# An attention and mixture-of-experts layer on one core: the first batch's scores after half the query projection, the second half's projections over three batches, two norms and all softmax normalisations on GpSimd

## What is computed

```python
x = x + attention(layernorm(x), ctx, Wq, Wkv, Wout)
x = x + ffn(layernorm(x), gate, gate_up, down, shared_gate_up, shared_down)

def attention(q, latent, Wq, Wkv, Wout):
    qp = q @ Wq.T                                  # 8 x 112 x 512
    k, v = split(latent @ Wkv.T)                   # latent is 8 x 375 x 128
    scores = einsum("bhqd,bhkd->bhqk", qh, kh) / sqrt(32)
    scores = where(tril, scores, lowest)           # row q sees keys 0..q, so 112 keys do
    attn = softmax(scores)
    return (attn @ vh) @ Wout.T
```

## Time and profile before

| | |
|---|---|
| median of 3 runs | 339.84 us (339.09 to 340.3) |
| the profiled execution | 340.88 us |
| its span, first to last instruction | 339.0 us |
| busy: PE, DVE, ACT, POOL | 323.1, 268.6, 232.4, 143.3 us |
| granted TensorE clock, mean | 0.991 |

### The profile page before, as it was taken

How to read it: one execution, slowest core, us unless ns; L and a number is a source line. 1 busy time by engine, 2 the same in 40 slices (tenths; PEclk the granted TensorE clock), 3 DMA queues, 4 the chain that set the end, 5 groups by cost and what they waited for, 6 DMA issues and landing times.

```text
span 339.0 us, 7041 instructions
## 1 busy us (share of the span) xinstructions
PE 323.1 (95%) x2285; PEld 279.3 (82%) x2285; DVE 268.6 (79%) x677; ACT 232.4 (69%) x582; POOL 143.3 (42%) x151
## 2 busy tenths in 40 slices
PE   7999998999999999999999999899999999999990
PEld 7898876777786798889888978789989999999980
DVE  4889779999756176876667998899999999999940
ACT  4666999999844134131225788788899899989830
POOL 3335475888842000352500005557772432432463
PEclk9999999999999999999999999999999999999996
DMA  7999300000005699598699965554455455556243
GB/s 227 380 338 380 139 3 3 3 3 3 0 2 198 248 367 370 237 300 289 224 271 253 251 244 98 102 117 104 90 111 131 90 96 125 114 92 113 50 48 45
DMA packets 32227, 53.03 MB, mean 156 GB/s; under 512 B 7488, under 2 KB 15808, under 8 KB 31168
## 3 DMA queue, kind: packets, MB, share of 16 engines
q1 hardware_dynamic: 24912, 43.31, 39.2%
q0 software_dynamic: 4576, 9.23, 15.9%
q10 hardware_dynamic: 2704, 0.04, 0.5%
HBM read 32.24 MB, written 16.92 MB: 145 GB/s over the span
## 4 chain that ended last, share of the span: by engine, by line
PE 74%; ACT 8%; DVE 5%; DMA 5%; POOL 3%; issue 2%; SPq 1%; POOLq 1%; DVEq 0%; ACTq 0%
PE bank L583 26%; PE bank L913 22%; PE bank L940 5%; ACT prob L1076 4%; PE bank L644 3%; PE bank L944 3%; PE bank L807 2%; PE bank L950 2%; PE bank L954 2%; DMA w_sg<-sguT 2%; DMA act_w<-act_e 2%; DMA w_kv<-wkvT 1%; PE bank L793 1%; PE bank L575 1%; PE bank L655 1%
## 5 line engine op out<-in xcount | busy, mean ns | idle before, releaser
L562 POOL DMA_INDIRECT out<-y_sb,dest x18 | 40.6, 2257 | 91.5 <-ACT y_sb L1256 49.7
L1333 DVE TENSOR_TENSOR gu_parts<-w_gu,gu_parts 128x704 fp32r<-128x704 f32 x84 | 76.0, 939 | 0.4 <-ACT gu_parts L1031 0.2
L1031 ACT ACTIVATE gu_parts<-w_gu 128x704 fp32r x84 | 66.1, 792 | 10.8 <-PE bank L913 9.7
L913 PE MATMUL bank<-gu_parts,xsT_hi 128*128 128x352 f32 x328 | 71.1, 338 | 0.0
L913 PEld LDWEIGHTS bank<-gu_parts,xsT_hi 128*128 128x128 f32 x328 | 54.3, 188 | 5.6 <-issue 4.3
L913 PE MATMUL bank<-gu_parts,xsT_lo 128*128 128x352 f32 x164 | 39.6, 323 | 0.0
L583 PE MATMUL bank<-x2T_hi,w_sg_lo 128*128 128x512 f32 (+1 forms) x88 | 32.6, 371 | 0.1
L583 PE MATMUL bank<-x2T_hi,w_sg_hi 128*128 128x512 f32 (+1 forms) x88 | 31.9, 363 | 0.0
L583 PE MATMUL bank<-x2T_lo,w_sg_hi 128*128 128x512 f32 (+1 forms) x88 | 31.9, 363 | 0.0
L445 POOL TENSOR_TENSOR prob<-prob,rrow 112x448 f32<-112x448 f32 x30 | 27.5, 934 | 9.9 <-DVE rrow L1383 9.8
L523 POOL DMA_INDIRECT xs_dram<-x2n,slot_i x14 | 13.9, 993 | 37.6 <-DVE eid L1631 33.6
(11 more groups left out here) (219 smaller groups left out, 826.3 us busy)
## 6 DMA issues: line engine op xcount, KB each, us to landing
w_gu<-guT SPq DMA_DIRECT2D x8, 1408.0 KB, 9.6
xs_dram<-no_row SPq DMA_DIRECT2D x1, 5460.0 KB, 19.7
xs_in<-xs_dram SPq DMA_DIRECT2D x21, 256.0 KB, 10.1
w_dn<-dnT SPq DMA_DIRECT2D x8, 512.0 KB, 7.9
act_w<-act_e SPq DMA_DIRECT2D x19, 176.0 KB, 2.1
w_sg<-sguT SPq DMA_DIRECT2D x10, 256.0 KB
w_dn<-dnT SPq DMA_DIRECT2D x8, 192.0 KB, 8.5
w_sd<-sdnT SPq DMA_DIRECT2D x5, 256.0 KB, 5.8
```

Of the source, the lines that this page charges most:

```text
L562: pool.indirect_dma_start(out=out[:, :], out_offset=bass.IndirectOffsetOnAxis(ap=dest[:, i, 0:1], axis=0), in_=y_sb[i % 2][:, :], in_offse ...
L913: ins = pe.matmul(dst[:, 0:F], xsT[x_][:, c, :], gu2[w_][:, c, f0:f0 + F], start=c == 0 and n == 0, stop=c == C - 1 and n == 2)
L1031: act.activation(dst, src, ACT.Copy).then_inc(s[sem], 1)
L1333: dve.tensor_tensor(lo_, src, hi_.bitcast(F32), ALU.subtract).then_inc(s[sem], 1)
```

## The change

First batch: `q_part` on the first 256 columns is moved out of PSUM at once (`put_qT_part`, semaphores `Qf` and `QTf`), and `scores(0)` runs after the first of the four second-column groups; it and `scores(1)` need only those 256 columns. The transposes of tiles 4 to 6 go to A, B and D instead of S[0..2]. Second half: before, `q_proj(1, 0..2)` and `k_proj(1, 0..2)` were done by the end of step 0 and the last of each in step 1; after, `q_proj(1, j)` runs at j = 0 and 1 in step 0, j = 2 in step 1 and j = 3 in step 2, and two of the `k_proj` in step 1. POOL writes the normalised rows of tiles 5 and 6 and multiplies all of batch 0; its two copies and subtractions of `w_o` move behind that. `sg_lo(0)`, `sd_lo(0)` and the copy `ident_f` move from before the attention to DVE's step 6. The core of the diff:

```diff
@@ gpsimd
-            pool.wait_ge(s["wsd_lo"], 1)
+            for n in range(BLK + 1, NX):
+                apply1(n)
+            for r in range(R):
+                normalised(0, r)
             pool.wait_ge(s["wo"], 16)
@@
-            for c in range(C // 2):
-                wo_lo(c)
-            normalised(0, 2)
             for b in range(NB):
-                normalised(b, 3)
+                if b >= 1:
+                    normalised(b, 3)
...
                 if b + 1 < NB:
                     normalised(b + 1, 0)
+                    if b == 0:
+                        for c in range(C // 2):
+                            wo_lo(c)
                     normalised(b + 1, 1)
@@ tensor
             def transposed(b, r):
-                if b == 0 and r < RP:
-                    pe.wait_ge(s["prob"], r + 1)
-                else:
-                    pe.wait_ge(s["prob_p"], R * b + r + 1 - RP)
+                pe.wait_ge(s["prob_p"], R * b + r + 1)
+                if b == 0 and r < 2:
+                    pe.wait_ge(s["xnT_lo"], BLK + 1 + r)
@@
             for j in range(C):
+                pe.wait_ge(s["QTf"], j + 1)
                 for c in range(C):
                     ins = q_part(c, j, second, bank[4 + j])
                 ins.then_inc(s["Q"], 1)
+                if j == 0:
+                    scores(0)
                 if j == 1:
-                    t1(4, S[0])
+                    pe.wait_ge(s["QT"], 1)
+                    t1(4, A)
                 if j == 2:
-                    t1(5, S[1])
-                    t1(6, S[2])
+                    pe.wait_ge(s["QT"], 2)
+                    t1(5, B)
...
             k_proj(1, 0, CC)
-            pe.wait_ge(s["xnT_hi"], NX)
-            pe.wait_ge(s["xnT_lo"], NX)
-            scores(0)
-            q_proj(1, 0, D)
-            q_proj(1, 1, B)
+            pe.wait_ge(s["QT"], C)
+            t1(6, D)
@@ in the loop over b, behind scores(b + 1)
+                if b in (1, 2):
+                    pe.wait_ge(s["QT"], C + b + 1)
+                    q_proj(1, b + 1, D)
+
+                transposed(b, 0)
+                transposed(b, 1)
                 if b == 0:
+                    pe.wait_ge(s["xnT_hi"], NX)
+                    pe.wait_ge(s["xnT_lo"], NX)
+                    q_proj(1, 0, D)
                     pe.wait_ge(s["KT"], C + 1)
                     k_proj(1, 1, CC)
...
                 transposed(b, 3)
+                if b == 0:
+                    pe.wait_ge(s["QT"], C + 1)
+                    q_proj(1, 1, D)
+                if b == 1:
+                    pe.wait_ge(s["KT"], C + 3)
+                    k_proj(1, 3, CC)
@@ scalar
-            for r in range(R):
-                exps(0, r)
-                if r == 0:
-                    put_kT(1, 0, CC)
-                if r == 2:
-                    put_qT(1, 0, D)
...
+            put_qT_part(3, second, "Q", "QT")
+            put_xnT(6, D)
+            exps(0, 2)
+            put_kT(1, 0, CC)
+            put_pT(0, 0)
+            put_pT(0, 1)
+            exps(0, 3)
+            put_qT(1, 0, D)
             for b in range(NB):
-                put_pT(b, 0)
-                if b < 2:
+                if b == 1:
+                    put_qT(1, 2, D)
+                if b >= 1:
+                    put_pT(b, 0)
+                if b == 1:
                     put_pT(b, 1)
@@ vector
             for b in range(NB):
...
                 if b + 1 < NB:
                     inverse(b + 1, 0)
+                if b == 2:
+                    put_qT(3, D)
                 if b >= 2:
                     put_pT(b, 1)
...
+                if b == NB - 2:
+                    sg_lo(0)
+                    sd_lo(0)
+                    dve.tensor_copy(ident_f[:, :], ident[:, :]).then_inc(s["idf"], 1)
                 if b >= 3:
                     x2T_lo(b - 3, CC)
```

More of the change, by code:

```diff
@@ L709, in _ @@
                         pe.wait_ge(s["KT"], j + 1)
-                    q_part(c, j, first, bank[4 + j])
+                    ins = q_part(c, j, first, bank[4 + j])
+                    if c == C - 1:
+                        ins.then_inc(s["Qf"], 1)
                 if c == 2:
@@ L745, in _ @@
                     shared_gu(0, 0, (0,))
+                if b in (1, 2):
[3 more added lines that the diff above has]
+                transposed(b, 1)
                 if b == 0:
+                    pe.wait_ge(s["xnT_hi"], NX)
+                    pe.wait_ge(s["xnT_lo"], NX)
+                    q_proj(1, 0, D)
                     pe.wait_ge(s["KT"], C + 1)
                     k_proj(1, 1, CC)
[L750 to L755, removed]
-                    pe.wait_ge(s["KT"], C + 2)
[L757 to L761, removed]
+                if b == 1:
+                    pe.wait_ge(s["KT"], C + 2)
                     pe.wait_ge(s["oT_hi"], 1)
                     pe.wait_ge(s["oT_lo"], 1)
-                    k_proj(1, 3, CC)
+                    k_proj(1, 2, CC)
                 if b >= 2:
@@ L1047, in put_qT, with put_qT_part @@
                 act.activation(qT[:, j, XC[k]], bank_[:, 0:WX[k]], ACT.Copy, scale=SCALE).then_inc(s["QT"], 1)
+            def put_qT_part(j, cols, of, to):
+                act.wait_ge(s[of], j + 1)
+                act.activation(qT[:, j, cols], bank[4 + j][:, cols], ACT.Copy, scale=SCALE).then_inc(s[to], 1)
             def put_kT(k, j, bank_):
@@ L1118, in _ @@
             put_xnT(3, S[3])
+            first, second = slice(0, 2 * P), slice(2 * P, 4 * P)
+            for j in range(C):
+                put_qT_part(j, first, "Qf", "QTf")
             ctx_hi(1)
[L1120 to L1129, removed]
-            for r in range(R):
-                exps(0, r)
-                if r == 0:
-                    put_kT(1, 0, CC)
-                if r == 2:
-                    put_qT(1, 0, D)
-            for b in range(NB):
-                put_pT(b, 0)
-                if b < 2:
+            put_qT_part(0, second, "Q", "QT")
+            sg_hi(0)
+            sd_hi(0)
+            exps(0, 0)
+            put_qT_part(1, second, "Q", "QT")
+            put_xnT(4, A)
+            exps(0, 1)
+            put_qT_part(2, second, "Q", "QT")
+            put_xnT(5, B)
+            put_qT_part(3, second, "Q", "QT")
[6 more added lines that the diff above has]
+            put_qT(1, 0, D)
+            for b in range(NB):
+                if b == 1:
+                    put_qT(1, 2, D)
+                if b >= 1:
+                    put_pT(b, 0)
+                if b == 1:
                     put_pT(b, 1)
@@ L1141, in _ @@
                     exps(b + 1, 0)
-                if b == 0:
-                    put_qT(1, 2, D)
                 if b < 2:
@@ L1388, in put_pT @@
                    .then_inc(s["probT_v"], 1)
-            def normalised(b, r):
-                inverse(b, r)
-                dve.wait_ge(s["rr"], R * b + r + 1)
-                dve.tensor_tensor(prob[r][:, :, :], prob[r][:, :, :],
-                                  rrow[:, r, :].unsqueeze(2).to_broadcast([SQ, C, SQ]), ALU.mult)\
-                   .then_inc(s["prob"], 1)
             whole = slice(None)
@@ L1453, in _ @@
             xnT_lo(3, S[3])
-            dve.tensor_copy(ident_f[:, :], ident[:, :]).then_inc(s["idf"], 1)
             dve.wait_ge(s["xrest"], 16)
@@ L1457, in _ @@
             stats1(5)
+            stats1(6)
+            dve.wait_ge(s["const"], 3)
+            masked(0, 0)
             apply1(4)
-            stats1(6)
-            apply1(5)
+            masked(0, 1)
             ctx_lo(1)
-            apply1(6)
-            xnT_lo(4, S[0])
-            xnT_lo(5, S[1])
-            xnT_lo(6, S[2])
-            sg_lo(0)
-            sd_lo(0)
-            dve.wait_ge(s["const"], 3)
-            for r in range(R):
-                masked(0, r)
-            normalised(0, 0)
-            normalised(0, 1)
+            masked(0, 2)
+            xnT_lo(4, A)
+            inverse(0, 0)
+            masked(0, 3)
+            xnT_lo(5, B)
+            inverse(0, 1)
+            xnT_lo(6, D)
+            masked(1, 0)
             inverse(0, 2)
-            put_qT(1, B)
-            masked(1, 0)
-            put_kT(1)
+            masked(1, 1)
             inverse(0, 3)
-            masked(1, 1)
             masked(1, 2)
             for b in range(NB):
-                if b == 1:
-                    put_kT(3)
+                if b < 2:
+                    put_kT(b + 1)
                 if b + 1 < NB:
                     inverse(b + 1, 0)
+                if b == 2:
+                    put_qT(3, D)
                 if b >= 2:
```

27 lines of the change are left out of this document (19 added, 8 removed).

## The result

| | before | after |
|---|---|---|
| median | 339.46 us (339.0 to 340.3, 4 runs) | 348.59 us (347.75 to 349.66, 4 runs) |
| the profiled execution, its span | 340.88, 339.0 us | 349.15, 347.0 us |
| busy: PE, DVE, ACT, POOL | 323.1, 268.6, 232.4, 143.3 us | 328.0, 268.6, 233.7, 150.5 us |
| granted TensorE clock, mean | 0.991 | 0.983 |

The change makes the kernel slower: ratio 1.0265, 95% interval [1.0243, 1.0287]. The prediction was 342.9 us, in the range 340.9 to 344.6; it was counted from the median of the three runs of before then at hand, 339.84. The direction was right, the size was not: +9.1 us where +3.1 was forecast.

The account below looks back on a forecast made before the run. PE was taken as the bound, with ACT nearly full too from 27 to 60 us. New holes 5.7 against 3.7 closed (+2.0) plus step 6's 1.1 gave +3.1 on 339.84: 342.9 us, range 340.9 to 344.6.

Parts of the forecast that it names:

- The hole of batch 2: PE's wait before `out_proj(0)` for DVE's last query copy, queued behind `inverse(3, 0)`: 2.7 us, the largest term.
- forecast 3.4: Batch 2's chain from the start of `transposed(2, 0)` through exponentials and DVE's query copy to PE: 3.4 us.
- That of batch 0: PE's new wait before `transposed(0, 3)`, released by POOL's normalisation: 1.55 us.
- +2.0: Net loss up to `scores(4)`: new holes of 5.7 us against 3.7 us of old holes closed.
- finish line: Start of `scores(4)`, at 57.46 us in the old order, where that order has become PE's alone.
- the releasers it named in this stretch: DVE's query copy (`qT`) ending batch 2's wait, POOL ending the one before batch 0's last transposes.
- the term of 1.1: Step 6: three moved DVE instructions delay `x2T_lo(3)` and PE's product; 1.9 less slack of 0.3 and 0.5: 1.1 us.
- the dearer sum of 1.9: Step 6's term if DVE's subtractions contend with POOL, 0.76 us more: 1.9 us, not adopted.
- a rival at 5%: Clock falls to 1.2 GHz after batch 2's wait, `out_proj` matmuls cost 2.1 us more, 345.0 us in all; 5%.

Follow-up runs that it names:

- kernel 2: Changed kernel with 24 unread identity transposes before `out_proj(0)`'s wait and 20 before step 6's product: 344.47 us, ratio 1.0134.
- 11: Kernel before with only `sg_lo(0)`, `sd_lo(0)` and `ident_f` moved ahead of `x2T_lo(3)` in step 6, POOL's `wsd_lo` wait dropped: 342.68 us, ratio 1.0091.
- 7: Kernel before with POOL's two subtractions for `w_o` moved behind `normalised(0, 3)`: 339.44 us, ratio 1.0006.
- kernel 3: Changed kernel with `sg_lo(0)` moved to DVE's step 0, `sd_lo(0)` and `ident_f` to step 7: 345.3 us, ratio 1.0178.
- 8: The kernel before, unchanged, run again for a second profile: 339.45 us.
- 12: The changed kernel, unchanged, run again for a second profile: 347.84 us.
- Kernel 4: Changed kernel with `put_qT(3)` ahead of DVE's reciprocal in step 2 and the shared-weight work moved out of step 6: 342.73 us, ratio 1.0093.
- 5: Kernel 4 with `q_proj(1, 2)` and `q_proj(1, 3)` both in step 1: 342.62 us, ratio 1.0106.
- 6: As 5, plus `q_proj(1, 1)` ahead of `transposed(0, 3)` and `put_qT(1, 0)` on DVE in step 0: 343.65 us, ratio 1.0134.
- 1: Changed kernel with `put_qT(3)` moved ahead of the reciprocal that waits for exponentials, on DVE in step 2: 345.23 us, ratio 1.0161.
- 9: Changed kernel with only the 24 unread transposes ahead of `out_proj(0)`'s wait: 345.01 us, ratio 1.0184.
- 10: Changed kernel with only the 20 unread transposes ahead of step 6's product: 345.84 us, ratio 1.0194.

## Why the prediction was wrong

**The waits of the attention: right.** The hole of batch 2 was forecast at 2.7 and is marked 2.25; from the start of the transposes at 51.77 to the matmul at 54.95 it is 3.18, forecast 3.4. That of batch 0 was forecast at 1.55 and is marked 1.17. With the clock kept up, `scores(4)` comes 47.83 - 45.90 = 1.9 us later (kernel 2), where the prediction had +2.0. Its sum to the finish line held, and so did the releasers it named in this stretch.

**Step 6: the term of 1.1, half of what it measured.** It measured 2.1 alone (11) and 4.1 - 1.9 = 2.2 in the changed kernel (2). The prediction had the price of contention before it (1.38 against 0.62), worked out the dearer sum of 1.9, and kept the lower since it had one pair of rows. The three instructions took 2.76 to 2.78, not 1.9, and the slack of PE and DVE was 0.65 (2.76 - 2.1), not 0.8. The rule of the Trainium skill, GPSIMD Engine Reference, section Specifications, that POOL and an instruction of DVE with two SBUF inputs contend, is what 7 and 11 show. The price is no constant: 0.73 to 0.76 for the instructions of 512 and 448 elements per partition here, 0.14 to 0.16 for `w_sg_lo` in step 6 and 2.8 for the same `w_sg_lo` in step 0 of kernel 3.

**The clock: left out of the sum, a rival at 5%.** This is the step that failed, with the size of step 6 beside it. The prediction put a loss after the 2.7 wait at 2.1 us and gave it 5%, because no row of before showed the array idle so long. Nor did any row show that it could idle so long at no cost: the longest wait within before's work, for an expert's activation weights, is 1.5. It was there in both profiles of the changed kernel and at both waits, 1.5 and 1.6 us by the ledger (3.1 together, against 2.8 by 2's profile), and 4.1 of the median with 2's fill; and the second loss, in step 6, was in none of the cases, as the wait was taken for 1.1 long. The rule named there, TensorE: Matmul & The Clock Gate, Part 1, in the Trainium skill, that the array returns to half rate when it idles, is what seven of the ten waits of this length show and three do not.

**The sum.** Of the +9.1 in the medians, 6.9 stand in the attention by the profiles: 1.9 of waits and closed holes up to `scores(4)` (forecast 2.0), 2.2 in step 6 (forecast 1.1) and 2.8 of clock (forecast nothing). Kernel 2's median, 344.47, says +5.0 with the clock kept up and 4.1 for the clock, so it lays more of the rest on the clock than the profiles do. The remaining 2.2 is shown by no stretch of the attention.

**What stays open.** The code of the expert tiles is not touched, yet PE loses 0.5 to 1.9 us there in all profiles of kernels that start from the changed one, waiting for a tile's activation weights from a DMA (`act_w`) or for what DVE makes of a late tile (`actT_split_lo`). Before's own profile had 1.5 of it, those of 7 and 8 none, 11 had 1.3. From the gate to the last product with gate and up weights it is 221.68, 219.66 and 219.51 in before, 7 and 8, and 220.53 in 11; in the kernels from the changed one it is 220.01 to 222.08, the changed one itself 222.08 and 221.61. By the first pair of profiles that is 0.4 of the loss, by the second (12 against 8) 2.1. It may be chance that falls differently or a shift of the transfers; no kernel here takes the two apart.

**Why undoing the parts did not pay.** Kernel 4 removes both long waits and is still at 1.0093, and 5 and 6 push the waits from batch 2 to batch 1. Part of that is their own: all three carry `w_sg_lo` at 4.0 to 4.4 us in DVE's step 0, which costs about 0.7 to 0.8 to `scores(4)` in 3 and 4 and holds the copy that 5 and 6 wait for. That ACT and DVE would be too full in this stretch in any order is therefore not shown. By the ledger the best of these orders reaches the gate 1.15 us behind before (5). No version here beats the kernel before.

## What to carry to other kernels

Price every new wait of the tensor engine twice: its length, and then the work behind it at half the clock; here a wait of 2 us cost 3.5 in most profiles, while waits up to 1.4 cost their length only in all of them, so that shortening a wait a little, or filling it with work that nobody reads, can be worth more than the wait. Before a subtraction with two inputs moves beside a busy GpSimd, take its duration from a row where both are at the very work that they will do: the same `w_sg_lo` took 1.22, 1.36 and 4.03 us in three places. And if a price is bounded by two rows, choose by the situation that the instruction will be in, not by the number of rows.

## What the runs showed of the hardware

The clock fell behind seven of ten waits of 1.96 to 2.25 us of PE (both profiles of the changed kernel twice; 1, 6 and 11 once), and not behind three of the same lengths (3, 9, 10), once with the very same instructions up to there. It did not fall behind any of twelve waits of 1.15 to 1.38 us in the attention, nor behind those of 1.3 to 1.5 us in the expert tiles (before, 6 and 11). Profiled runs without a loss in the attention have a mean clock of 0.991 to 0.995, with one 0.987 to 0.989, with two 0.983. By that measure the changed kernel lost it twice in all five runs (0.983 to 0.986), kernel 3 once in three of four (0.987 to 0.990) and kernel 5 once in three of six, though its profile has no wait over 1.4: the profiles alone do not prove such waits safe. By the share of 0.50 in the windows it fell between 0.2 us before the array resumed (12, the first wait: 0.51 over 54 to 56, resumed at 54.23) and 1.1 us after (the changed kernel's second), and it was back some 3 us later. In POOL's row the contention shows as well: four products took 4.59 and 4.60 beside DVE's two subtractions, and 3.61 in the step before.
